# The last GRU layer's state: turned by DMA and added on POOL and DVE, in place of TensorE's fp32 transposes

## What is computed

```python
h = relu(layernorm(x))
for i in range(3):                       # three GRU layers
    m = h @ weight[i]
    aggr = einsum('bst,bsd->btd', A, m)
    h = gru_cell(aggr, h, w_ih, w_hh, b_ih, b_hh)
x = x + h                                # the residual that the change touches
h = relu(layernorm(x))
Wh = h @ W.T
x = x + softmax(leaky_relu(s1 + s2), masked) @ Wh   # s1, s2: dot products of Wh
```

## Time and profile before

| what | value |
|---|---|
| median of 3 runs | 1824.64 us |
| the profiled execution's own time | 1824.46 us |
| its span, first to last instruction | 1822.6 us |
| mean granted clock of TensorE | 0.991 of full speed |
| busy: PE, DVE, ACT, POOL | 98%, 78%, 56%, 19% of the span |
| one pair in the loop | about 109.4 us |

### The profile page before, as it was taken

The page is one execution under the profiler, slowest core; times in us unless marked ns, Lnnn a source line. Parts: engine busy times, 40 slices in busy tenths (PEclk is TensorE's granted clock), DMA queues, the critical chain, the costliest instruction groups (busy, mean ns, idle before and its releaser), DMA issues.

```text
span 1822.6 us, 32181 instructions
## 1 busy us (share of the span) xinstructions
PE 1779.6 (98%) x10492; PEld 945.1 (52%) x10492; DVE 1417.3 (78%) x2801; ACT 1022.5 (56%) x1822; POOL 354.7 (19%) x778
## 2 busy tenths in 40 slices
PE   6999999999999999999999999999999999999993
PEld 5444555545555454555545555454555545555552
DVE  6667788787887877788787887877788787887866
ACT  5556556555555555556555555555556555555552
POOL 1022130311303122130311303122130311303100
PEclk9999999999999999999999999999999999999997
DMA  3322332323323223322323324223322323323221
GB/s 104 76 64 65 70 75 58 90 66 69 87 40 104 57 59 91 69 75 58 89 66 68 87 39 105 57 60 90 69 75 58 88 67 68 88 39 88 41 69 41
DMA packets 325789, 128.87 MB, mean 71 GB/s; under 512 B 241280, under 2 KB 325760, under 8 KB 325760
## 3 DMA queue, kind: packets, MB, share of 16 engines
q1 hardware_dynamic: 325760, 128.50, 30.0%
HBM read 52.96 MB, written 16.78 MB: 38 GB/s over the span
## 4 chain that ended last, share of the span: by engine, by line
PE 96%; DVE 1%; issue 1%; ACT 0%; POOL 0%; DVEq 0%; POOLq 0%; ACTq 0%
PE z_bank L320 27%; PE r_bank L320 27%; PE hn_bank L320 14%; PE in_bank L320 14%; PE s_bank L320 3%; PE w_bank L320 3%; PE nb_bank L334 2%; PE nb_bank L335 2%; PE t_bank L762 2%; PE t_bank L776 1%; ACT relu_att L272 0%; DVE dot_terms L947 0%; PE nb_bank L320 0%; ACT u_hi L858 0%; DVE stats_att L250 0%
## 5 line engine op out<-in xcount | busy, mean ns | idle before, releaser
L837 ACT ACTIVATE n_out<-n_pre,bih 128x512 f32<-128x512 f32 x192 | 138.0, 719 | 238.9 <-DVE n_pre L901 238.6
L320 PE MATMUL hn_bank<-ht_s,wh_hi 128*128 128x512 f16 x768 | 228.4, 379 | 1.7 <-PEq L428 1.7
L846 ACT ACTIVATE ht_s<-ht 128x512 f16<-128x512 f32 x128 | 80.6, 630 | 264.5 <-DVE ht L917 264.5
L320 PE MATMUL r_bank<-ht_s,wh_hi 128*128 128x512 f16 x768 | 228.5, 379 | 0.0
L320 PE MATMUL z_bank<-ht_s,wh_hi 128*128 128x512 f16 x768 | 228.4, 379 | 0.0
L353 DVE TENSOR_TENSOR nb_lo<-nb_bank,nb_hi 128x512 f16<-128x512 f32 x192 | 131.1, 683 | 84.1 <-ACT nb_hi L349 84.0
L896 DVE SCALAR_TENSOR_TENSOR n_pre<-tanh_r,hn_b 128x512 f32<-128x512 f32 x192 | 146.3, 762 | 62.9 <-ACT tanh_r L832 59.0
L297 POOL TENSOR_TENSOR ln_gnn<-stats_gnn 128x4 f32<-128x4 f32 x32 | 18.6, 582 | 893.2 <-DVE stats_gnn L250 893.2
L832 ACT ACTIVATE tanh_r<-r_bank,b_rz,down 128x512 f32<-128x512 f32 x192 | 147.2, 767 | 65.9 <-PE r_bank L320 65.7
L827 ACT ACTIVATE hn_b<-hn_bank,b_hn,down 128x512 f32<-128x512 f32 x192 | 147.9, 770 | 57.0 <-PE hn_bank L320 57.0
L910 DVE SCALAR_TENSOR_TENSOR diff<-ht,n_out 128x512 f32<-128x512 f32 x192 | 132.0, 687 | 38.8 <-ACT n_out L837 38.5
(11 more groups left out here) (190 smaller groups left out, 3939.4 us busy)
## 6 DMA issues: line engine op xcount, KB each, us to landing
x_in<-in_x_dram SPq DMA_DIRECT2D x32, 512.0 KB, 3.8
x_res<-in_x_dram SPq DMA_DIRECT2D x32, 512.0 KB, 4.0
out_dram<-x_out SPq DMA_DIRECT2D x32, 512.0 KB, 5.2
adj_in<-in_adj_dram SPq DMA_DIRECT2D x32, 256.0 KB, 4.0
adj_att<-in_adj_dram SPq DMA_DIRECT2D x32, 256.0 KB, 4.3
h_s<-ht_s SPq DMA_TRANSPOSE x128, 3.0
ht_s<-h_s SPq DMA_TRANSPOSE x64, 3.2
raw_ih<-in_L_gnn_w_ih_dram SPq DMA_DIRECT2D x2, 384.0 KB, 3.7
```

What stands on the lines that cost most here:

```text
L320: last = nc.tensor.matmul(bank_ap, w, d, start=start and i == 0, stop=stop and i == len(todo) - 1)
L837: nc.scalar.activation(n_out[c][:], n_pre[c][:], ACT.Tanh, bias=bih[:, 4 + c:5 + c]).then_inc(n_ready, 1)
L846: nc.scalar.activation(ht_s[layer % 2][a][:, c, 0, :], ht[a][:, c, :], ACT.Copy, scale=HSCALE).then_inc(ht_hi_ready, 1)
```

## The change

For 15 of the 16 pairs `residual` has no part on PE any more. Behind each `update` of the last layer come three new stages, and `residual` is now fed by them: `split_last` (ACT makes the high half, DVE the low half of the last state, in `ht_s[1]`), `turn_last` (SP turns both halves by one DMA transpose into `h_last`), `add_last` (POOL adds the two turned halves into `h_node`), and `residual` (DVE scales `h_node` and adds `x_res`, in one operation). The last pair keeps the transposes on PE.

`whole_state` now waits for `last_lo_ready` (the low half of the last state is made) where it waited for PE's transposes. The places in the table move too:

```diff
 SIDE = {
-    (0, 0): [("residual", 1, 0, -1), ("update", 1, 2, 1, -1)],
-    (0, 1): [("load_gnn", 0, 1)],
+    (0, 0): [("update", 1, 2, 1, -1), ("split_last", 1, 1, -1), ("turn_last", 1, 1, -1), ("add_last", 1, 0, -1)],
+    (0, 1): [("load_gnn", 0, 1), ("apply_att", 0, -1), ("residual", 1, 0, -1)],
-    (0, 3): [("residual", 1, 1, -1), ("split_att", 0, -1)],
+    (0, 3): [("add_last", 1, 1, -1), ("split_att", 0, -1)],
-    (0, 6): [("stats_att", 1, -1)],
+    (0, 6): [("residual", 1, 1, -1), ("stats_att", 1, -1)],
...
-    (4, 4): [("update", 0, 2, 0, 0)],
+    (4, 4): [("update", 0, 2, 0, 0), ("split_last", 0, 0, 0), ("turn_last", 0, 0, 0)],
...
-    (4, 7): [("gather", 1, 0, -1)],
-    (5, 0): [("residual", 0, 0, 0), ("update", 0, 2, 1, 0)],
-    (5, 1): [("gather", 1, 1, -1)],
+    (4, 7): [("gather", 1, 0, -1), ("add_last", 0, 0, 0)],
+    (5, 0): [("update", 0, 2, 1, 0), ("split_last", 0, 1, 0), ("turn_last", 0, 1, 0)],
+    (5, 1): [("gather", 1, 1, -1), ("residual", 0, 0, 0)],
...
-    (5, 3): [("residual", 0, 1, 0), ("attend", 1, 1, -1), ("load_att", 1, 0), ("store", 1, -1)],
-    (5, 4): [("update", 1, 2, 0, 0)],
-    (5, 5): [("neighbours", 0, 0, 1, 1), ("stats_att", 0, 0)],
-    (5, 6): [("apply_gnn", 1, 1)],
-    (5, 7): [("split_gnn", 1, 1), ("first_transpose", 1, 0, 1), ("first_transpose", 1, 1, 1), ("apply_att", 0, 0)],
+    (5, 3): [("add_last", 0, 1, 0), ("attend", 1, 1, -1), ("load_att", 1, 0), ("store", 1, -1)],
+    (5, 4): [("update", 1, 2, 0, 0), ("split_last", 1, 0, 0), ("turn_last", 1, 0, 0)],
+    (5, 5): [("neighbours", 0, 0, 1, 1)],
+    (5, 6): [("apply_gnn", 1, 1), ("residual", 0, 1, 0), ("stats_att", 0, 0)],
+    (5, 7): [("split_gnn", 1, 1), ("first_transpose", 1, 0, 1), ("first_transpose", 1, 1, 1)],
```

The new code on SP, ACT, DVE and POOL, and the changed waits:

```diff
+                def turn_last(p, a, c):
+                    if not after_gates(p):
+                        sp.wait_ge(last_lo_ready, per_chunk(p, a, c))
+                        sp.sem_inc(sp_step, 1)
+                        wait_reached(sp, h_node_ready, per_chunk(p, a, c) - 2)
+                        sp.sem_inc(sp_step, 1)
+                        sp.dma_start_transpose(h_last[:, c].rearrange("p s b t -> p (s b) t"),
+                                               ht_s[LAYERS % 2][a][:, c].rearrange("p s t -> p (s t)")).then_inc(
+                                                   h_last_landed[a][c], 16)
...
+                def split_last(p, a, c):
+                    if not after_gates(p):
+                        act.wait_ge(h_ready, per_gate(p, a, LAYERS - 1, c))
+                        nc.scalar.activation(ht_s[LAYERS % 2][a][:, c, 0, :], ht[a][:, c, :],
+                                             ACT.Copy, scale=HSCALE).then_inc(last_hi_ready, 1)
...
+                def split_last(p, a, c):
+                    if not after_gates(p):
+                        dve.wait_ge(last_hi_ready, per_chunk(p, a, c))
+                        nc.vector.scalar_tensor_tensor(ht_s[LAYERS % 2][a][:, c, 1, :], ht[a][:, c, :], HSCALE,
+                                                       ht_s[LAYERS % 2][a][:, c, 0, :], ALU.mult,
+                                                       ALU.subtract).then_inc(last_lo_ready, 1)
...
                     dve.wait_ge(x_res_loaded[a], per_load(p))
-                    dve.wait_ge(res_t_done, per_chunk(p, a, c))
                     part = x_res[a][:, :, c * P:(c + 1) * P]
+                    if not after_gates(p):
+                        dve.wait_ge(h_node_ready, per_chunk(p, a, c))
+                        nc.vector.scalar_tensor_tensor(part, h_node[c][:], 1.0 / HSCALE, part, ALU.mult,
+                                                       ALU.add).then_inc(x1_ready, 1)
+                        return
+                    dve.wait_ge(res_t_done, 2 * a + c + 1)
...
                 def whole_state(p, a, c):
                     pool.wait_ge(first_ht_landed[a][c], per_load(p))
-                    wait_reached(pool, res_t_done, per_chunk(p - 1, a, c))
+                    wait_reached(pool, last_lo_ready, per_chunk(p - 1, a, c))
...
+                def add_last(p, a, c):
+                    if not after_gates(p):
+                        pool.wait_ge(h_last_landed[a][c], per_load(p))
+                        wait_reached(pool, x1_ready, per_chunk(p, a, c) - 2)
+                        nc.gpsimd.tensor_tensor(h_node[c][:], h_last[:, c, 0], h_last[:, c, 1],
+                                                ALU.add).then_inc(h_node_ready, 1)
```

More of the change, by code:

```diff
@@ L610, in graph_blocks @@
         diff = [sb(f"diff{c}", [P, T], F32) for c in range(2)]
+        h_last = sb("h_last", [P, KC, 2, GROUP, P], F16)
+        h_node = [sb(f"h_node{c}", [P, GROUP, P], F32) for c in range(KC)]
         score = sb("score", [P, GROUP, P], F32)
@@ L642, in graph_blocks @@
         res_t_done = sem("res_t_done")
+        h_node_ready = sem("h_node_ready")
+        last_hi_ready, last_lo_ready = sem("last_hi_ready"), sem("last_lo_ready")
+        h_last_landed = [[sem(f"h_last_landed{a}{c}") for c in range(KC)] for a in range(2)]
         gather_done, s2_done, attend_done = sem("gather_done"), sem("s2_done"), sem("attend_done")
@@ L715, in _ @@
                     "load_gnn": lambda p, a: load_gnn(sp, p, a), "store": store, "load_att": load_att,
-                    "probs_transpose": probs_transpose,
+                    "probs_transpose": probs_transpose, "turn_last": turn_last,
                     "transpose": transpose, "first_transpose": lambda *which: first_transpose_sp(sp, *which)})
@@ L756, in residual @@
                 def residual(p, a, c):
+                    if not after_gates(p):
+                        return
                     pe.wait_ge(h_ready, per_gate(p, a, LAYERS - 1, c))
-                    wait_reached(pe, x1_ready, per_chunk(p, a, c) - 1)
+                    pe.wait_ge(x1_ready, per_chunk(p, a, c) - 1)
                     if a == 0 and c == 0:
-                        wait_reached(pe, sum_ready, per_group(p - 1, 1))
+                        pe.wait_ge(sum_ready, per_group(p - 1, 1))
                     for b in range(GROUP):
@@ L883, in _ @@
                     "apply_gnn": lambda p, a: apply_gnn(act, p, a), "apply_att": apply_att, "split_state": split_state,
+                    "split_last": split_last,
                     "neighbours": lambda *which: neighbours_act(act, *which), "split_att": split_att,
@@ L1008, in _ @@
                     "stats_att": stats_att,
-                    "update": update, "split_state": split_state,
+                    "update": update, "split_state": split_state, "split_last": split_last,
                     "residual": residual, "split_att": split_att, "dots": dots,
@@ L1024, in _ @@
                 all_pairs(pool, lambda *step: None, {
-                    "first_transpose": whole_state,
+                    "first_transpose": whole_state, "add_last": add_last,
                     "stats_gnn": lambda p, a: norm_factors(pool, "gnn", p, a, relu_gnn_ready),
```

7 lines of the change are left out of this document (4 added, 3 removed).

## The result

The changed kernel takes **1972.66 us** (median of 5 runs, 1970.67 to 1973.16) against 1824.64 (1824.15 to 1825.98) for the kernel before in the same series: ratio 1.081, 95% interval 1.079 to 1.082. It is slower, as forecast, but by 148 us instead of 93, and so outside the range, whose top was 1946.

A forecast was written before the change was run, and what follows sets the result against it. The prediction took PE, busy 98% of the span, as the bound. Its terms, 3.45 + 2.25 + 0.55 + 0.6 - 0.65 = 6.2 us a pair, 15 times, gave 93 us on 1824.46: 1917.5 us, range 1850 to 1946.

The forecast's parts named there:

- 3.45, the lateness at the end of `split_gnn`: End of slot 5: ACT's norm starts at 16.1 instead of 12.60, so DVE's `split_gnn` ends 3.45 us late.
- the first place, in slot 4, costs nothing: Slot 4, chunk 0 of group 0: added work is free, since DVE stands idle over 5 us later there.
- POOL's third place in the queue: Slot 0: the last state's addition stands third on POOL, so DVE's residual waits and `n_pre` starts 2.25 us later still.
- the race: Slot 0: POOL's next addition may take the SBUF port before DVE's residual; 1.1 us or nothing, 0.55 taken.
- T: The end of DVE's `split_gnn`, from which the prediction counted slot 0's times.
- 0.6, the residual of chunk 1: Slot 0 to 1: this residual moves from DVE's idle time to dense time, 0.6 us more a pair.
- -0.65, the cover: Slot 1: the turned state lands 0.65 us before PE's neighbours need it at 1044.12, which hides that much lateness.
- Rival 3: More clashes of POOL additions with DVE, or a later transpose landing: 8 us a pair, 1944 us; chance 0.12.
- Rival 1: Covers hold and PE stays the bound, given DVE lateness below 0.65 us at slot 1's split: 1798 us; chance 0.10.

The follow-up runs named there:

- e9: Kernel with additions ahead of whole_state, splits one step later, second residual in (0,3); in (4,5) `neighbours` now stands ahead of `apply_gnn`: 1855.57 us.
- w3: Kernel before with group 0's state turned as 16-bit words (ACT, SP), no POOL addition or split; ACT's `nb_hi` ahead of the norm in (4,5): 1812.55 us.
- e8: Changed kernel with additions ahead of whole_state, splits one step later, and chunk (1,1)'s addition and residual moved to (0,3): 1882.91 us.
- e5: Changed kernel with additions ahead of whole_state; POOL's last-state additions cut to 4 columns, residual reading the high half alone: 1884.83 us.
- e10: e8 with POOL's additions cut to 4 columns and the residual reading the high half alone: 1864.68 us.
- e11: e9 with POOL's addition of chunk (1,0) moved from (5,7) to the start of (5,6), ahead of the attention factors: 1863.68 us.

## Why the prediction was off

The direction, the engine and the order of events were right: PE at 92%, DVE idle ahead of L967 for POOL's sum at both places (1.63 us in slot 5, 3.69 in slot 0), the PE waits that it named (the one for `n_pre` only twice, 1.1 us in all), and the landing at the end that sets the period. What failed is the size of what it added up. Its own sum, 3.45 + 2.25 + 0.55 + 0.6 - 0.65 = 6.2 us a pair, stands against 9.65:

- **3.45, the lateness at the end of `split_gnn`: 4.9.** The sum let ACT's norm set this moment, and ACT was as late as forecast: its norm starts at 1095.05, which is 1016.18 on the clock of before (16.1 forecast), and its high half ends at 1098.37. DVE comes to `split_gnn` 1.4 us later, at 1099.76, because the residual of chunk 1 and behind it `stats_att`, both in (5,6) now, stand ahead of it. That queue held two pieces that were missing. The addition of chunk (0,1) runs at 1094.75, and the reset product at 1094.76 takes 1.68 us instead of 0.69: a second clash, 1.0. The prediction placed the first on the split (it is there: 1.22 us at 1082.09) and did not go through the other additions. The rest, nearly 0.5, is there already ahead of slot 5: "the first place, in slot 4, costs nothing" failed. `nb_lo` at 1075.36 is 996.49 on the clock of before, against 996.00 there. DVE's 5 us without work in that slot are no room, since they are a wait for `nb_hi`, and ACT makes that behind the norm; e9 and w3 show that the order alone made them. The trace shows where the 0.5 arises, though no run isolates it: in POOL's small operations ahead of that norm, one of which grew beside the reset product that the new split had pushed back. ACT after, then POOL before and after:

```profile
1097.22 1.15 ACT L285 ACTIVATE h_s<-relu_gnn 128x512 f16<-128x512 f32 x2
```

```profile
990.85 1.01 POOL L312 TENSOR_TENSOR ln_gnn<-ln_gnn,consts 128x4 f32<-128x4 f32 x1
```

```profile
1069.76 1.45 POOL L312 TENSOR_TENSOR ln_gnn<-ln_gnn,consts 128x4 f32<-128x4 f32 x1
```

- **2.25 + 0.55, POOL's third place in the queue and the race: 3.9.** This step failed by an omission, about 0.8 of the difference. It began POOL's `whole_state` at the landing, T + 3.62; POOL was still at the attention factors until T + 4.65, because the change moves `stats_att` from (5,5) to (5,6). The instructions of a moved step are counted on every engine, and eleven small ones on POOL, 5.8 us together, were not. The race is the other 0.4: it came out at 0.93 (1.62 against 0.69), where 0.55 was taken. POOL's second addition started at 1108.97, the residual at 1109.04. By the rule of the Trainium skill that the prediction weighed there ("SBUF — State Buffer", "Who interferes with whom"), the first to issue keeps the port, and the trace agrees: the three DVE operations that met an addition in this period took 1.62, 1.68 and 1.22 us, and each ended 0.54 to 0.56 us after POOL did.
- **0.6, the residual of chunk 1: 0.9**, up to the update of slot 1; e8 puts 0.87 on it.
- **-0.65, the cover: -0.4.** Of the difference, 0.16 is a reading: 1044.12 is the fourth of the eight neighbour matmuls, and the one that waits for the landing is the first, at 1043.96. And 0.3 more is lost at the next landing, in slot 2, which the sum took to be covered.

By size, the second clash comes first (1.0; e5 measures such a clash at 0.9), then the factors (0.8) and the half microsecond from slot 4. Rival 3, that the clashes are more, names the kind of the first; its 8 us a pair were too few as well.

What the experiments say of the parts, on the way from after to before: additions ahead of `whole_state` 59 us, the split one step later 18, the second residual back in idle time 13, `nb_hi` ahead of the norm 27, and 31 for what is left, additions, split and the factors' chain. This is one path, and in another order the parts would come out otherwise; e10 gives 18 us for the additions at a point where e9's move isn't made. How the last 31 divide wasn't settled: e11 only shows that the sum's wait in slot 0 can't be had alone, since the chain through the factors is as late.

Rival 1 (covers hold) fell by far. Its condition, a lateness under 0.65 us a pair at the landing, is what w3 meets: PE waits for no landing there.

## What to carry to other kernels

When work is taken off an engine that never idles, price first what the replacement does to the latest of its feeders: here the 26 us saved on TensorE ended as 148 lost, behind a VectorE that was busy for 78% of the span and had no cover in three slots. Move each step with all that hangs on it, the small instructions of an in-order queue too, and ask of every wait that you remove what is next to being as late. A version that gives the feeder no extra work, for the half of the places that have cover, and with one idle order put right, brings 12 us.
